# Attention output in a two-layer transformer: moves within SBUF in place of TensorE transposes

## The reference

```
mod = silu(c) @ w_mod + b_mod                      # 6 rows of 288 for each sample
xn  = ln(x) * (1 + sc_msa) + sh_msa
q, k, v = split(xn @ w_qkv + b_qkv)                # 16 heads of 18
attn = softmax(q @ k.T * 18 ** -0.5)
o   = (attn @ v).merge_heads() @ w_proj + b_proj
x   = x + g_msa * o
h   = gelu((ln(x) * (1 + sc_mlp) + sh_mlp) @ w1 + b1)     # 288 -> 1152
x   = x + g_mlp * (h @ w2 + b2)
```

## Time and profile before

| | us |
|---|---|
| runs, median of 3 | 2603.22 (2599.84 to 2608.05) |
| profiled execution, its own time | 2611.21 |
| its span, first to last instruction | 2609.3 |
| PE busy in the span | 2456.2 (94%) |
| VectorE, ScalarE, GpSimd busy | 1817.3, 1553.7, 685.5 |
| mean granted TensorE clock | 0.975 of full speed |

### The profile page before, as it was taken

How to read it: one execution, slowest core, us unless ns; L and a number is a source line. 1 busy time by engine, 2 the same in 40 slices (tenths; PEclk the granted TensorE clock), 3 DMA queues, 4 the chain that set the end, 5 groups by cost and what they waited for, 6 DMA issues and landing times.

```text
span 2609.3 us, 58469 instructions
## 1 busy us (share of the span) xinstructions
PE 2456.2 (94%) x22115; PEld 2070.3 (79%) x22115; DVE 1817.3 (70%) x3637; ACT 1553.7 (60%) x2856; POOL 685.5 (26%) x937
## 2 busy tenths in 40 slices
PE   5579999999999999999999999999999999999998
PEld 3347888888888888888788788888888887888878
DVE  6367777777777777777766776676777676767664
ACT  3256666666666666666665665565656565656553
POOL 2012233233233233323321222221222222212222
PEclk7779999999999999999999999999999999999999
DMA  4775664664655555565555455456445644554431
GB/s 134 131 174 115 120 114 96 108 106 92 106 102 97 101 102 102 97 105 97 121 90 93 111 97 86 73 86 97 77 76 92 94 75 75 97 90 74 76 61 40
DMA packets 222775, 252.95 MB, mean 97 GB/s; under 512 B 21928, under 2 KB 206160, under 8 KB 221984
## 3 DMA queue, kind: packets, MB, share of 16 engines
q1 hardware_dynamic: 208504, 216.24, 48.6%
q10 hardware_dynamic: 13992, 32.96, 4.1%
HBM read 107.38 MB, written 32.31 MB: 54 GB/s over the span
## 4 chain that ended last, share of the span: by engine, by line
PE 68%; SPq 10%; DMA 10%; DVE 6%; issue 3%; ACT 2%; ACTq 0%; POOL 0%; POOLq 0%; DVEq 0%
PE psum L733 17%; PE psum L831 8%; DMA attn_k_stack<-attn_qk_hi 8%; SPq L1300 7%; PE psum_exp L807 6%; PE psum_exp L733 6%; PE psum_max L733 6%; PE psum L898 5%; PE psum L900 5%; PE psum L899 5%; PE psum_max L820 4%; SPq L1305 3%; DVE attn_maxima L1072 3%; PE psum L740 3%; DVE attn_qk_centred L1110 2%
## 5 line engine op out<-in xcount | busy, mean ns | idle before, releaser
L934 ACT ACTIVATE attn_probs<-psum_exp 128x1024 f32<-128x1024 f32 x512 | 523.5, 1022 | 430.4 <-PE psum_exp L807 426.1
L1072 DVE TENSOR_REDUCE attn_maxima<-psum_max 128x4 f32<-128x1024 f32 x512 | 620.2, 1211 | 133.7 <-PE psum_max L820 133.4
L1236 POOL TENSOR_TENSOR mlp_x<-mlp_x,mlp_gated 128x288 f32<-128x288 f32 x128 | 102.5, 801 | 1121.5 <-DVE mlp_gated L1089 1121.5
L733 PE MATMUL psum<-attn_ln_split,w_qkv_split 128*128 128x256 f32 (+3 forms) x2240 | 340.9, 298 | 9.6 <-DVE attn_ln_split L1178 3.2
L898 PE MATMUL psum<-mlp_w_fc_hi,mlp_hidden_hi 128*128 128x288 f32 x1152 | 341.6, 297 | 2.3 <-DVE mlp_w_fc_lo L720 1.1
L899 PE MATMUL psum<-mlp_w_fc_lo,mlp_hidden_hi 128*128 128x288 f32 x1152 | 340.2, 295 | 0.0
L900 PE MATMUL psum<-mlp_w_fc_hi,mlp_hidden_lo 128*128 128x288 f32 x1152 | 340.0, 295 | 0.0
L733 PEld LDWEIGHTS psum<-attn_ln_split,w_qkv_split 128*128 128x128 f32 (+3 forms) x2240 | 285.9, 183 | 62.5 <-issue 15.0
L831 PE MATMUL psum<-attn_probs,attn_v 128*20 128x256 f32 x4096 | 279.1, 391 | 1.1 <-ACT attn_probs L934 1.1
L820 PE MATMUL psum_max<-attn_k_stack,attn_q_stack 62*128 62x256 f32 x2048 | 216.9, 289 | 59.8 <-DMA attn_k_stack<-attn_qk_hi 47.3
L807 PE MATMUL psum_exp<-attn_q_stack,attn_k_stack 64*128 64x256 f32 x2048 | 260.4, 332 | 7.9 <-DMA attn_q_stack<-attn_neg_max_lo 3.7
(11 more groups left out here) (165 smaller groups left out, 4261.0 us busy)
## 6 DMA issues: line engine op xcount, KB each, us to landing
attn_q_stack<-attn_qk_hi SPq DMA_DIRECT2D x256, 128.0 KB
attn_k_stack<-attn_qk_hi SPq DMA_DIRECT2D x256, 128.0 KB
mlp_gate_and_gated_bias<-modulation ACTq DMA_DIRECT2D x64, 288.0 KB, 3.2
attn_qk_squares<-qk_rstd SPq DMA_DIRECT2D x32, 512.0 KB
attn_q_stack<-attn_qk_lo SPq DMA_DIRECT2D x128, 128.0 KB
attn_k_stack<-attn_qk_lo SPq DMA_DIRECT2D x128, 128.0 KB
attn_x<-in_x_dram SPq DMA_DIRECT2D x32, 288.0 KB, 7.2
attn_gate<-modulation SPq DMA_DIRECT2D x64, 144.0 KB, 3.4
```

The source lines that it names most:

```text
L733: mm = q.matmul(to, lhs, rhs, start=(i == 0), stop=(i == 6))
L934: q.activation(probs[r][:], ps_exp[:], ACT.Exp, scale=SCORE_SCALE).then_inc(S["exps"], 1)
L1072: q.tensor_reduce(maxes[g % 2][:, p // QUARTER, :, p % QUARTER, :], ps_max[:].rearrange("p a (t n) -> p a t n", t=TT), AX.X, ALU.max).then ...
L1236: q.tensor_tensor(xt, xt, gated2[:], ALU.add).then_inc(S["added2"], 1)
```

## The change

The output of attention no longer passes through transposes. Each group's `o_t` block (128 rows, four heads in strips of 32) is moved within SBUF by one transfer of 128 KB to 32 rows of a new buffer `attn_o_and_sums`: rows 4i to 4i+3 become one row with four blocks of 256 tokens. For this V is laid out with 32 columns for a head as 8 rows of 4: channels 0 to 7, 8 to 15, the last two channels three times over and two zeros, and a one in every fourth place. So the fourth block of the new buffer holds the row sums beside every row of channels. ScalarE forms the reciprocal as exp(-ln(sum)), VectorE multiplies all three blocks in one instruction, and the split into high part and rest works from SBUF. The projection weights are laid out by head to match, with their last block full at 128 rows, and the bias on rows of its own.

Work in slots (modulo 16): the four moves are issued by SP in slots 11, 12, 14 and 2, reciprocal in slot 5, product in 6, high part in 7 (layer 0) or 8, rest in 8 or 9. The second layer norm's scaling goes from slot 6 to 7, its split from 7 to 8 (layer 0) or 12 (layer 1). The two buffers `attn_neg_max_hi` and `attn_neg_max_lo` become single.

```diff
-VW = HD + 2
+VW = 32
+EIGHT = 8
-O_TR, O_BACK = 18, (22, 23)
+O_MOVE, O_RECIP, O_NORM, O_HI, O_LO = (11, 12, 14, 18), (21, 21), (22, 22), (23, 24), (24, 25)
-STATS2, RSTD2, NORM2, REST2, TR2, Y2, SPLIT2, GATE2_AT = 31, 32, 35, 36, 37, 38, 39, (46, 48)
+STATS2, RSTD2, NORM2, REST2, TR2, Y2, SPLIT2, GATE2_AT = 31, 32, 35, 36, 37, 39, (40, 44), (46, 48)
...
+        def arrange_proj(q, l):
...
+            for i in range(3):
+                q.dma_start(proj_d[l][:, 2 * i:2 * i + 2, :], w.rearrange("(h d) n -> h d n", d=HD)[:, 2 * EIGHT:HD, :]).then_inc(S["proj_rest", l], 16)
+            q.dma_start(proj_d[l][:, 6:8, :], bias.broadcast_to([HEADS, 2, C])).then_inc(S["proj_rest", l], 16)
...
-                        for grp in range(GROUPS):
-                            mm = q.transpose(bank[:, grp * P:grp * P + P], o_t[:, grp, t * P:t * P + P], ident[:])
-                        mm.then_inc(S["o_turned"], 1)
...
-                            mm = q.matmul(bank[32 * i:32 * i + VW, 0:N], v_sb[g % V_RING][:, t, grp * PV_HEADS + i, :],
+                            mm = q.matmul(bank[32 * i:32 * i + VW, 0:N], v_sb[g % V_RING][:, t, grp * PV_HEADS + i, :, :].rearrange("p r c -> p (r c)"),
...
-                if (g := due(T, O_BACK)) is not None:
-                    q.wait_ge(S["o_rest"], g + 1)
-                    ab, last = bank_of(("back", g, 0)), bank_of(("back", g, 1))
-                    mm_ab, mm_last = to_channels(q, ab, last, o_sb)
...
                     if grp == 0 and g > 0:
-                        q.wait_ge(S["o_turned"], TT * g)
+                        q.wait_ge(S["o_moved"], 16 * GROUPS * g)
                     q.activation(o_t[:, grp, :], psum[PV_BANK][:, 0:N], ACT.Copy).then_inc(S["o_copied"], 1)
...
+                if (g := due(T, O_RECIP)) is not None:
+                    q.wait_ge(S["o_moved"], 16 * GROUPS * (g + 1))
+                    q.activation(o_sb[:, 3, :], o_sb[:, 3, :], ACT.Ln).then_inc(S["o_log"], 1)
+                    q.wait_ge(S["o_log"], g + 1)
+                    q.activation(o_sb[:, 3, :], o_sb[:, 3, :], ACT.Exp, scale=-1.0).then_inc(S["o_recip"], 1)
+                if (g := due(T, O_HI)) is not None:
+                    q.wait_ge(S["o_norm"], g + 1)
...
+                    q.activation(o_acts[:, 0:2, :], o_sb[:, 0:2, :], ACT.Copy).then_inc(S["o_hi"], 1)
+                    q.activation(o_tmp[:], o_sb[:, 2, :], ACT.Identity, scale=1.0, bias=bias_row[:]).then_inc(S["o_hi"], 1)
...
-                        q.activation(v_sb[g % V_RING][:, t, :, 0:HD], psum[banks["v", g, t][0]][:, 0:C].rearrange("p (h d) -> p h d", d=HD),
-                                     ACT.Copy).then_inc(S["v_ready"], 1)
+                        q.activation(runs[:, :, 0:2, :], heads[:, :, 0:2 * EIGHT].rearrange("p h (c r) -> p h c r", r=EIGHT), ACT.Copy)
+                        q.activation(runs[:, :, 2, 0:6].rearrange("p h (u d) -> p h u d", u=3),
+                                     heads[:, :, 2 * EIGHT:HD].rearrange("p h (u d) -> p h u d", u=1).broadcast_to([P, HEADS, 3, 2]), ACT.Copy).then_inc(S["v_ready"], 1)
...
+                if (g := due(T, O_NORM)) is not None:
+                    q.wait_ge(S["o_recip"], g + 1)
+                    q.tensor_tensor(o_sb[:, 0:3, :], o_sb[:, 0:3, :], o_sb[:, 3:4, :].broadcast_to([P, 3, N]), ALU.mult).then_inc(S["o_norm"], 1)
...
+                for grp in range(GROUPS):
+                    if (g := due(T, O_MOVE[grp])) is not None:
+                        if grp == 0 and g > 0:
+                            q.wait_ge(S["o_lo"], 2 * g)
+                        q.wait_ge(S["o_copied"], GROUPS * g + grp + 1)
+                        q.dma_start(o_sb[VW * grp:VW * grp + VW, :, :], o_t[:, grp, :]).then_inc(S["o_moved"], 16)
```

207 lines of the change are left out of this document (108 added, 99 removed).

## The result

The change makes the kernel slower: 2706.35 us (median of 4 runs, 2697.56 to 2717.07) against 2603.35 us for the kernel before in the same comparison, a ratio of 1.040 with a 95% interval of 1.036 to 1.044. The forecast was 2570 us, and the range ended at 2616.

The account below looks back on a forecast made before the run. Layer 0 was taken as bound by PE's work, layer 1 by the stack moves' landing plus PE's work behind it. Terms: -55 - 6 + 28 = -33 us from 2603, forecast 2570 us, range 2538 to 2616.

Parts of the forecast that it names:

- some ten short instructions: Start of the kernel: these, one more load and four small weight arrangements counted at nothing, with 5 us either way.
- The fourth move: SP's queue, ahead of the last three stack moves: delays the landing by 0.5 us, between bounds of 0.4 and 1.0.
- the dear move of the second rival: Fourth move costs as much as a stack move, 1.0 us; 36 us more, 2606 us, no change; chance 0.17.
- the halving by the rows written to: Fourth move writes 32 rows where a stack move writes 16, so takes half of its 1.0 us.
- The landing and the rest, layer 1: Last stack move lands 20.1 us after SP's first stack issue; 17.6 us follow, 19.1 with a fall of the clock.
- one of the two causes I had named: Behind layer 1's landing: ScalarE's logarithm and exponential ahead of exponentials, VectorE's product ahead of a maximum; gain possibly 0, taken 0.4 us.
- The clock: Layer 1: PE's wait grows to 2.4 us, a 1.5 us fall in each of 18 steps, 15 more than now.
- The rival in which the clock holds: At PE's 2.4 us waits in layer 1 the clock mostly stays at 2.4 GHz; 26 us less, 2544 us; chance 0.20.
- Layer 0: 27 steady steps each 2.04 us shorter (0.97 + 0.60 + 0.57 - 0.1), 55 us in all.
- The product with V: PE's matmuls with 32 stationary columns for 20: taken as 0 extra, up to 12 us kept for the range.
- ScalarE becoming what PE waits for: Slots 5 to 9: ScalarE's additions delay PE's scores, up to 1.3 us in 60 steps, 78 us, 2648 us; chance 0.14.
- The start and the mixed steps: Start counted at nothing, 5 us either way; six steps around the change of layers gain 1.0 us each, 6 us.

Follow-up runs that it names:

- e14: The changed kernel with its one-column constants merged and padded, so that large tiles stand at the addresses of the kernel before: 2636.6 us.
- e1: The changed kernel with its four moves issued for the first step only (output not the reference's): 2612.4 us.
- e8: The kernel before with the four moves added beside its transposes, to a spare tensor that nobody reads: 2657.2 us.
- e12: The changed kernel whose fourth move takes half of each row, 64 KB, to the same 32 rows from the second step on: 2654.5 us.
- e4: The changed kernel with the product by the reciprocals and the split of the output one slot later: 2703.7 us.
- e6: The changed kernel with the second layer norm's modulation and split in layer 0 back in their earlier slots: 2703.8 us.
- e7: The changed kernel with 20 identity transposes on PE ahead of its wait for the stacks in each step of layer 1: 2667.0 us.
- e16: The kernel before with 256 bytes of padding among its small constants: 2600.1 us.
- e18: The kernel before with 128 bytes of padding just behind the stacks, so only V and later tiles move up: 2604.0 us.
- e17: The kernel before with 128 bytes of padding just ahead of the q and k stacks, so the stacks and all behind move up: 2627.0 us.
- e13: The kernel before with 128 bytes of padding among its small constants, every later tile up to V shifted: 2636.5 us.
- e5: The changed kernel with only its fourth move limited to the first step, the other three staying: 2620.3 us.
- e3: The kernel before with 10 of the 14 output transposes left out from the second step on, no move added: 2596.7 us.

## Why the prediction was wrong

**What bounds the kernel** was read rightly: layer 1 by landing and rest, layer 0 by PE.

**The step that failed first is one that is not there**: the sum has no term for where tiles stand. Of the small additions the working says "some ten short instructions", and it puts them at nothing; the four new constants also move every large tile up to V by 128 bytes. Taking that back gives 70 of the 103 us (e14). It is not a share that can be added to the others, since taking the moves away gives 94 (e1). The changed kernel without its moves is 10 us behind the kernel before (e1), with its moves and the addresses of before 36 us (e14), and with both 103. In part it is the clock that makes the two cost more together than apart: it falls in 15, 13 and 23 of the 25 steps. With the addresses restored the whole kernel stands at 2637 us: my range would still have missed it, by 21 us.

A step of layer 1 was forecast 0.97 us longer and with the addresses restored is 1.10 us longer (38.86 for 37.76). That is in part luck. The landing was right, 20.1 us, but the rest of the step where the clock holds was forecast at 17.6 us and is 18.3, and against that stand 13 falls of 1.0 us and not 18 of 1.5.

**The fourth move**, 0.5 us in the sum, is the dear move of the second rival: it added 0.9 us to the flood in e8, 0.7 to 0.8 in e14 and 0.9 to 1.2 in the changed kernel. The step that failed is the halving by the rows written to. What halved the price is half the bytes (e12). The Trainium skill's rule (SBUF — State Buffer, Door 1: The DMA port swizzle), by which 32 partitions reach twice the ports of 16, did not show here: these prices of 128 KB to 32 rows are nearer to the 1.0 us of a stack move to 16 than to half of it. Where the stacks stand as before, the move added a little less to the landing than to the flood, 0.7 us in e8 and 0.6 in e14. The rival had the mechanism and a time of 2606 us, which did not have the addresses either.

**The landing and the rest, layer 1.** Forecast 20.1 us for the landing, measured 21.6, or 21.0 to 21.1 in the executions of e4, e6 and e7. That is 1.5 to 2.4 us later than in the kernel before, which has 19.5, or 19.2 in e16 and e18. The addresses are 0.7 to 0.9 of it (e17 and e13 against e18 and e16) and the fourth move 0.7 (e8) to 1.6 (after against e5). Whether anything is left over can't be told within the scatter. In the changed kernel SP issues `attn_gate` 19.8 us behind its first stack issue, ahead of the landing, and in the kernel before 20.7 us, behind it; that these 144 KB slow the last moves was not tried. The rest of the step was forecast at 17.6 us and is 18.26 where the clock holds, 0.24 us more than the 18.02 of before in spite of six transposes fewer. The first half of the miss is e3's finding: ScalarE's exponentials hold that stretch at 18.0 to 18.1 with or without them. In the other PE waits for a maximum that stands behind the product on VectorE, one of the two causes I had named. The timeline of ScalarE, VectorE and PE in the changed kernel, in the step that lands at 1780.16:

```profile
1782.06 0.40 ACT L977 ACTIVATE attn_o_and_sums<-attn_o_and_sums 128x256 f32<-128x256 f32 x1
1782.49 0.42 ACT L979 ACTIVATE attn_o_and_sums<-attn_o_and_sums 128x256 f32<-128x256 f32 x1
1782.95 0.96 DVE L1181 TENSOR_TENSOR attn_o_and_sums<-attn_o_and_sums 128x768 f32<-128x768 f32 x1 [0.29 <-ACT attn_o_and_sums L979]
1783.82 1.22 DVE L1095 TENSOR_REDUCE attn_maxima<-psum_max 128x4 f32<-128x1024 f32 x1
...
1785.10 0.50 PE L861 MATMUL psum_max<-attn_k_stack,attn_q_stack 62*128 62x256 f32 x4 [0.43 <-DVE attn_maxima L1095]
```

Logarithm, exponential, product, maximum, and 0.43 us of PE's wait behind them. In e7, where the clock holds, nearly every step of layer 1 has this wait:

```profile
PE psum_max L865 <- DVE attn_maxima L1099: 9.9, 23, 0.4
```

But e4, which puts the product behind that maximum, got nothing back, because the exponentials came next. So this wait is what the trace shows, and not a price that can be saved by itself.

**The clock.** Right in kind and in the price of one fall, 1.5 us forecast and 1.5 measured (19.75 in the steps with a fall less 18.26). The wait was forecast at 2.4 us and was 3.5, since the landing slipped by 2.1 and not by 0.5, and so 23 of the 25 steps fell and not 18. The rival in which the clock holds is refuted by the counts above: of 58 waits of 2.0 to 2.5 us 45 were followed by a fall. e7 shows that the wait is the cause, since it only puts matmuls into the wait, and the clock holds in 23 of 25 steps.

**Layer 0** was forecast at 36.6 us and is 37.79. PE's work fell by 1.27 us a step for 1.57 (the wait of 0.57 ahead of `attn_o`'s transposes did go). New waits took 1.0 us back: for the stacks 0.42 us, forecast as 0.1, and for the maximum, ahead of the transposes of the maxima, 0.71 us for 0.20. This second one is the split that now runs beside GpSimd's (e6). The working has VectorE with "about as much to do": it asks how much and not beside what. Of the 1.2 us missed the moves are 0.6 (e1).

**The product with V** was right. The groups of the 23 steps of layer 0 (busy us, mean ns of one), after, and then before:

```profile
L872 PE MATMUL psum<-attn_probs,attn_v 128*32 128x256 f32 x1472 | 98.5, 385 | 0.0
```

```profile
L831 PE MATMUL psum<-attn_probs,attn_v 128*20 128x256 f32 x1472 | 97.6, 382 | 0.0
```

0.9 us in 23 steps for twelve more stationary columns, which is under 3 us in all 64 steps where the range kept 12.

**ScalarE becoming what PE waits for** (0.14) did not happen in the changed kernel (4.2 us in 25 steps), but e3, e4 and e6 each ran into it as soon as anything was shifted. "430 us idle" was a poor argument against it: the idle time lies elsewhere.

**The start and the mixed steps**, counted at nothing and at -6 us, cost 9.8 and 24.8 us. Without moves they cost 2.0 and 5.7 (e1), and with the addresses restored 7.2 and 14.3 (e14). Why the moves cost more there was not tried.

## What to carry to other kernels

When a change adds or resizes even a small tile, compare where the tiles that DMAs write to stand, modulo 256 bytes, before looking for any cause in the schedule; padding ahead of them costs nothing to try, and here it was worth more than the change itself. A transfer that was put into a saturated train of transfers cost about its bytes at the train's rate: put it behind the one that somebody waits for. And work that PE loses ahead of a wait is no gain but a longer wait. After most waits of 1.5 us and more the clock was lower here, and matmuls that only fill the wait gave back 39 us.

## What the runs showed of the hardware that was not expected

- A flood of moves of 128 KB from 128 rows to 16, in pieces of 1 KB, runs in layer 1 at 1.06 to 1.07 us a move where the written tile begins 32 bytes behind a multiple of 256 in its partitions, and at 1.00 to 1.02 us at 160 bytes (e13 and e17 against e16 and e18, and the kernels with shifted and with restored addresses in the table). 256 bytes more make no difference. Other places were not tried. A shift of what is read as well made no difference to the pace (e13 against e17), though e13 loses 35 us and e17 22.
- The Trainium skill (DMA: Bandwidth & Descriptors, How a descriptor splits into AXI transactions) says that a transfer is cut at multiples of 256 bytes and that the bytes ahead of an unaligned start are fetched too and cost. The period agrees with e16. The sign does not: by that rule a piece of 1 KB would be cheaper at 32 bytes than at 160, and it was dearer. The rule is told of reads, and what was shifted in e17 is written.
- An instruction of VectorE with two inputs in SBUF took 1532 ns beside one of GpSimd's of 1.29 us, and 481 ns alone.
- A matmul of 128 rows by 256 columns takes as long with 32 stationary columns as with 20 (385 and 382 ns by the profile's records).
- Of 280 steps of layer 1 in which PE waited less than 1.5 us, one had a fall of the granted clock; of 94 with over 2.5 us, 86. In the changed kernel a fall cost 0.4 to 1.8 us.
